# Seeding a PSUM bank from ScalarE instead of TensorE, and moving softplus's last sum from VectorE to TensorE in more tiles, in a selective-scan and mixture-of-experts layer

## What is computed

```
dt = softplus(ts @ W_dt.T + b_dt)
state = state * exp(dt * A) + (dt * u) * B        # u is x after convolution and silu
y = einsum(state, C)                              # over the 16 states
y = y + x * D                                     # the skip term
y = y * silu(gate)
s = y @ W_out.T
```

## Time and profile before

| | |
|---|---|
| three runs, median | 1090.31 us (1086.61 to 1090.49) |
| span of the profiled execution | 1086.8 us |
| time of the profiled execution outside the span | not in the profile; its span is 0.2 us above the fastest of the runs and 3.5 us below the median |
| mean granted clock of PE over the span | 0.911 of 2.4 GHz |
| chain that ended last, by engine | DVE 36%; PE 22%; POOL 15%; issue 12%; DMA 9%; ACT 4% |

### The profile page before, as it was taken

The page is one execution under the profiler, slowest core; times in us unless marked ns, Lnnn a source line. Parts: engine busy times, 40 slices in busy tenths (PEclk is TensorE's granted clock), DMA queues, the critical chain, the costliest instruction groups (busy, mean ns, idle before and its releaser), DMA issues.

```text
span 1086.8 us, 10255 instructions
## 1 busy us (share of the span) xinstructions
PE 872.1 (80%) x2774; PEld 323.8 (30%) x2774; DVE 1022.8 (94%) x1044; ACT 733.8 (68%) x1285; POOL 926.3 (85%) x365
## 2 busy tenths in 40 slices
PE   9944569798889998988656778989788997778576
PEld 5321123233223433333112223333223342223122
DVE  6779999999999999999999999899999999999998
ACT  3655567787787667766775667778767566676574
POOL 0629899999989889989889989798998978998995
PEclk9976788999989999999967879999999999799789
DMA  9355586556476665666743554766548566565714
GB/s 331 120 161 199 107 268 232 212 198 232 167 274 240 232 238 207 170 182 210 204 164 122 185 181 152 274 242 227 190 165 287 188 224 232 184 225 182 280 33 151
DMA packets 78089, 219.26 MB, mean 202 GB/s; under 512 B 15824, under 2 KB 17232, under 8 KB 71376
## 3 DMA queue, kind: packets, MB, share of 16 engines
q1 hardware_dynamic: 58096, 166.67, 44.7%
q10 hardware_dynamic: 12672, 31.46, 7.8%
q0 software_dynamic: 7264, 20.47, 6.9%
HBM read 176.85 MB, written 41.72 MB: 201 GB/s over the span
## 4 chain that ended last, share of the span: by engine, by line
DVE 36%; PE 22%; POOL 15%; issue 12%; DMA 9%; ACT 4%; SPq 2%; DVEq 0%; ACTq 0%; POOLq 0%
DVE sc_ps L1174 16%; POOL drive L567 10%; DVE drive L1174 6%; PE x_ps L1466 6%; DMA rep<-rep_rows 5%; DVE drive L1184 3%; PE f_ps L1419 3%; POOL drive L580 3%; PE y_ps L1434 3%; DMA x_slot<-xn_rows,slot_tok 2%; PE dt_ps L1394 2%; DVE x_ps L1113 2%; PE x_ps L1329 1%; PE x_ps L1351 1%; SPq L382 1%
## 5 line engine op out<-in xcount | busy, mean ns | idle before, releaser
L567 POOL TENSOR_TENSOR drive<-rep,b_all 128x2048 f32<-128x2048 f32 x127 | 575.8, 4538 | 44.1 <-DMA rep<-rep_rows 40.7
L799 ACT ACTIVATE sc_ps<-rep,a_neg 128x512 f32<-128x512 f32 x512 | 332.0, 681 | 86.2 <-DVE drive L1184 57.3
L1434 PE MATMUL y_ps<-drive,stack 128*32 128x512 f32 x1024 | 156.1, 687 | 89.7 <-DVE drive L1184 62.8
L1184 DVE TENSOR_TENSOR drive<-sc_ps,c_all 128x1024 f32<-128x1024 f32 x177 | 216.8, 1225 | 5.9
L1174 DVE TENSOR_TENSOR_SCAN sc_ps<-sc_ps,state,drive 128x512 f32<-128x512 f32 x178 | 218.4, 1273 | 3.8 <-ACT sc_ps L799 3.2
L1174 DVE TENSOR_TENSOR_SCAN sc_ps<-sc_ps,drive 128x512 f32<-128x512 f32 x176 | 205.3, 1212 | 5.5 <-ACT sc_ps L799 4.4
L580 POOL TENSOR_TENSOR drive<-drive,c_all 128x1024 f32<-128x1024 f32 x79 | 186.4, 2360 | 6.1 <-ACT state L778 6.1
L1419 PE MATMUL f_ps<-w_ring,xT_slot 128*128 128x512 f32 x368 | 176.5, 624 | 12.1 <-ACT xT_slot L811 12.1
L1394 PE MATMUL dt_ps<-xnT,w_g 128*128 128x512 f32 x232 | 117.8, 655 | 20.5 <-ACT dtu L766 20.4
L1419 PEld LDWEIGHTS f_ps<-w_ring,xT_slot 128*128 128x128 f32 x368 | 71.5, 201 | 118.3 <-issue 118.0
L1174 DVE TENSOR_TENSOR_SCAN drive<-sc_ps,state,drive 128x512 f32<-128x512 f32 x78 | 95.5, 1266 | 2.8 <-ACT sc_ps L799 2.8
(11 more groups left out here) (200 smaller groups left out, 1093.8 us busy)
## 6 DMA issues: line engine op xcount, KB each, us to landing
rep<-rep_rows SPq DMA_DIRECT2D x128, 512.0 KB, 6.7
w_ring<-wring SPq DMA_DIRECT2D x46, 1024.0 KB, 5.6
rep_rows<-dtu ACTq DMA_DIRECT2D x32, 512.0 KB, 3.3
slot_rows<-y_slot ACTq DMA_DIRECT2D x46, 256.0 KB
w_g<-wg_in SPq DMA_DIRECT2D x32, 256.0 KB, 2.7
w_x<-wx_in SPq DMA_DIRECT2D x24, 256.0 KB
xn_rows<-rep SPq DMA_DIRECT2D x16, 256.0 KB, 2.2
b_all<-bc_rows SPq DMA_DIRECT2D x16, 256.0 KB, 4.3
```

The costliest lines, as they stand in the source:

```text
L567: pool.tensor_tensor(drive[:, m % RING, :, :], rep[:, n % 2, :, 1, :], b_all[:, q:q + 1, :].broadcast_to([P, NR, TC]), ALU.mult).then_inc( ...
L799: act.activation(sc[:, r, :], rep[:, n % 2, r, 0, :], ACT.Exp, scale=a_neg[:, lo:lo + 1]).then_inc(decay_ok, 1)
L1184: dve.tensor_tensor(drive[:, m % RING, 2 * h:2 * h + 2, :], sc[:, 2 * h:2 * h + 2, :], c_all[:, q:q + 1, :].broadcast_to([P, 2, TC]), ALU. ...
L1434: last = pe.matmul(y_ps[CH * r:CH * (r + 1), :], stack[:, :], drive[:, m % RING, r, :], start=False, stop=(m % NQ == NQ - 1))
```

## The change

Three edits. The skip term is put into `y_ps` by one ACT instruction per tile (Copy with the scale D, 128x512), which waits for `gated`; PE waits for it (`skip_ok`) and then adds its sums onto it. Only tile 0 keeps the diagonal product. The Relu of a sum on PE is made in place in `dt_ps`, and PE adds three products onto it, not four onto a cleared bank. And `VECTOR_LOG` loses the tiles 2, 3, 16, 17, 19, 28, 29 and 31, so that 17 tiles, not 9, have their sum on PE.

```diff
-VECTOR_LOG = (0, 1, 2, 3, 4, 5, 7, 8, 10, 11, 12, 16, 17, 18, 19, 21, 23, 24, 26, 27, 28, 29, 31)
+VECTOR_LOG = (0, 1, 4, 5, 7, 8, 10, 11, 12, 18, 21, 23, 24, 26, 27)
...
                 if pe_log(k):
-                    act.activation(t_r[:, :], dt_ps[:, :], ACT.Relu).then_inc(relu_ok, 1)
+                    act.activation(dt_ps[:, :], dt_ps[:, :], ACT.Relu).then_inc(relu_ok, 1)
...
-            def diagonal(n):
-                if n:
-                    act.wait_ge(skip_mm, n)
-                act.activation(diag[:, :], ident[:, :], ACT.Copy, scale=dsk[:, n % NT:n % NT + 1]).then_inc(diag_ok, 1)
+            def diagonal():
+                act.activation(diag[:, :], ident[:, :], ACT.Copy, scale=dsk[:, 0:1]).then_inc(diag_ok, 1)
+
+            def skip(n):
+                if n == 0:
+                    return
+                c, t = divmod(n, NT)
+                act.wait_ge(gated, n)
+                act.activation(y_ps[:, :], xy[:, c % 2, t, :], ACT.Copy, scale=dsk[:, t:t + 1]).then_inc(skip_ok, 1)
...
-                diagonal(n)
+                if n == 0:
+                    diagonal()
                 if t < NT - 1:
                     keep_rows(n + 1)
...
                 decays(m + 1, 1)
+                skip(n)
                 copy_slot_T(b, first_slot)
...
-                pe.matmul(dt_ps[:, :], ident[:, :], t_e[:, :], start=True, stop=False)
-                pe.matmul(dt_ps[:, :], ident[:, :], t_w[:, :], start=False, stop=False)
-                pe.matmul(dt_ps[:, :], ident[:, :], t_l[:, :], start=False, stop=False)
-                pe.matmul(dt_ps[:, :], ident[:, :], t_r[:, :], start=False, stop=True).then_inc(log_mm, 1)
+                pe.matmul(dt_ps[:, :], ident[:, :], t_e[:, :], start=False, stop=False, skip_group_check=True)
+                pe.matmul(dt_ps[:, :], ident[:, :], t_w[:, :], start=False, stop=False, skip_group_check=True)
+                pe.matmul(dt_ps[:, :], ident[:, :], t_l[:, :], start=False, stop=True, skip_group_check=True).then_inc(log_mm, 1)
...
             def skip(n):
-                c, t = divmod(n, NT)
-                pe.wait_ge(diag_ok, n + 1)
                 if n:
-                    pe.wait_ge(gated, n)
-                pe.matmul(y_ps[:, :], diag[:, :], xy[:, c % 2, t, :], start=True, stop=False).then_inc(skip_mm, 1)
+                    pe.wait_ge(skip_ok, n)
+                    return
+                pe.wait_ge(diag_ok, 1)
+                pe.matmul(y_ps[:, :], diag[:, :], xy[:, 0, 0, :], start=True, stop=False)
```

More of the change, by code:

```diff
@@ L271, in scan_moe @@
         scaled, comb_ok, comb_last = sem("scaled"), sem("comb_ok"), sem("comb_last")
-        diag_ok, skip_mm = sem("diag_ok"), sem("skip_mm")
+        diag_ok, skip_ok = sem("diag_ok"), sem("skip_ok")
         x_mm, x_ev = sem("x_mm"), sem("x_ev")
@@ L1434, in sums @@
                     last = pe.matmul(y_ps[CH * r:CH * (r + 1), :], stack[:, :], drive[:, m % RING, r, :],
-                                     start=False, stop=(m % NQ == NQ - 1))
+                                     start=False, stop=(m % NQ == NQ - 1), skip_group_check=m >= NQ)
                 last.then_inc(sum_ok, 1)
```

## The result

The changed kernel took 1104.09 us, the median of 4 runs (1099.47 to 1104.93), against 1089.35 for the kernel before (1086.61 to 1090.49): a ratio of 1.0125, 95% interval 1.0098 to 1.0151. It is slower: the ratio, estimated from all the runs, gives 13.6 us, the medians 14.7. The forecast was 1100, slower, with 1082 to 1107 as its range. The profiled execution has a span of 1102.1 us, against 1086.8.

A forecast was written before the change was run, and what follows sets the result against it. DVE led at 94% busy, but the chain passed to POOL, `rep` and PE in places. Terms 0.7 + 3.4 + 3.3 + 4.0 = 11.4 us on 1086.8 gave 1098.2, put at 1100 us as the median; range 1082 to 1107.

The forecast's parts named there:

- DVE's 16.7 us: Three DVE instructions of 0.69 to 0.70 us leave each of eight tiles, 2.1 us a tile, 16.7 us in all.
- The rule of the most occupied engine: Trace-analysis advice to optimise the engine with highest occupancy first; by it the change is worth its DVE time.
- Tile 16, forecast +3.4: Sum made in tile 15 stands behind the gate's projection; DVE stands 8.6 us; +3.4 us (2 to 6).
- Tile 19, forecast +3.3: Sum made in tile 17 stands behind twelve out_tile products, moving the gate's projection, `rep` and POOL by +3.3 us.
- Tiles 2 and 3, +0.7: Sums made in tiles 0 and 1 at PE clock 0.50; dt of tile 2 later; +0.7 us (-2 to +2).
- tiles 28, 29, 31, +4.0: Sums in tiles 26 and 29 stand behind PE's sums waiting for POOL; +4.0 us (3 to 5.8).
- The skip term, forecast 0, from -3 to +4: ACT's seed fits its idle 0.71 us before the copy; expert products gain 0.1 us; counted 0, from -3 to +4.
- My fourth rival: Slower by more: seed keeps `y_ps` closed longer, 0.7 us a tile in half of 31, 11 us, 1111; chance 0.07.
- The faster one: DVE is the bound and its 16.7 us come off: 1073.6, or 1083 with half the stalls; chance 0.21 together.
- No change: Stalls as forecast but larger slack behind them, tiles 2, 3, 17 and 29 pay the rest: 1086 to 1095; chance 0.22.

The follow-up runs named there:

- e7: The kernel before with the changed kernel's 17 sums on PE and the in-place maximum, but the skip term still by diagonal product: 1094.48 us, ratio 1.0045.
- e11: The kernel before with 15 sums on PE (tiles 16 and 19 left on DVE), the in-place maximum and the diagonal product: 1088.45 us, ratio 0.9988.

## Why the prediction was right, and where it wasn't

The sign, the size (1104.1 against 1100) and, for tiles 16 and 19, the mechanism held: DVE came to wait at the places named, and these two stalls are most of the loss. The skip term and the price of the other six tiles did not hold. Step by step:

**DVE's 16.7 us.** 17.9 went, and its share fell to 91%. The waits for the last product rose by 18.3. The rule of the most occupied engine would have made the kernel faster; it is slower.

**Tile 16, forecast +3.4.** Right. The stall was 9.06 us against 8.6; gate 14 comes 7.1 us later than gate 13 did, and 3.7 of that are given back by gate 16: 3.4. Over the eight traces with this sum on PE it is 2.9 on average; the five without it gained 1.5, so the tile is worth 4.3 against the version without it, and 6.5 by putting it back, with an uncertainty of 4. The changed kernel's further 3.6 us at gate 13 are tile 12's, shown above; whether the seed or scatter brought them stays open.

**Tile 19, forecast +3.3.** Right by the traces: 2.9 us from gate 16 to gate 18 in the seven with it in its place, 0.2 in the five without. Putting it back gave 5.7, with the same uncertainty. Both tiles together are 10.0 us with the seed and 6.2 with the diagonal product (1.0045 less 0.9988), on the two sides of the 6.7 that I had summed; each is uncertain by 4, so that the seed makes these stalls dearer is possible and not shown.

**Tiles 2 and 3, +0.7, and tiles 28, 29, 31, +4.0.** The waits of 3.47 and 3.62 us at tiles 26 and 29 are where I said. But the six tiles other than 16 and 19 together cost 0.9 us with the seed, with an uncertainty of 4, and I had 4.7. The part on tiles 28, 29 and 31 is uncertain in itself: the traces with them on PE lost 3.4 us after gate 18 on average, from -4.0 to +10.2, those without 0.5, while the timed runs give 1.6 with an uncertainty of 5. Tile 17, whose sum had room, is in these six too.

**The skip term, forecast 0, from -3 to +4.** This is the step that failed. The runs put it at 2.7 to 8.7 us. I wrote that the seed fits into ACT's idle 0.71 us, from a tile whose transposes came late. There it does, but the products gain nothing: they begin 0.77 us after the transposes in both kernels, not 0.1 earlier. Where the transposes come early, ACT has no such idle time, the seed pushes the copy back, and the products begin 2.2 us after the gate instead of 1.6. And I asked what the diagonal product costs the path, not what PE does in its place. In the kernel before PE stands 20.7 us for the gate ahead of the diagonal products and 12.1 for the copy behind them, 32.8 in all; in the changed kernel it stands 52.9 in one piece each time, and behind the longest pieces the products run partly at 1.2 GHz. My fourth rival had the seed as the cause of a further loss, by 11 us through the sums that wait for `y_ps`. Those waits exist, 22.2 us of PE's weight loads in 7 places. No run separates them from the clock, so how the seed's cost divides between the two stays open.

So the total was near the mark partly because errors met: along one path from the kernel before to the changed one the runs give +2.7 for the seed, +0.9 for six tiles and +10.0 for two, 13.6 in all, where I had 0, 4.7 and 6.7. That the sum came out within 5 us of the measured time is in part luck.

**Rivals.** The faster one asked for stalls of tiles 15 and 17 under 4 us together; they are 9.06 and 5.34. "No change" asked for more slack behind them; there was less.

No version beat the kernel before. The nearest is e11, the diagonal product kept and tiles 16 and 19 left on DVE, at 0.9988 (0.9962 to 1.0013): the work it takes from DVE in six tiles is worth nothing that can be measured.

## What to carry to other kernels

Before work is moved off the fullest engine, look at each place for what stands ahead of it in the other engine's list, and for what the waiting engine wants first: here two places of eight made nearly the whole loss of the sums, and moving them ahead shortened one wait by 1.6 us and passed the other on to another consumer. A TensorE instruction that is off the path may still be worth its place when it splits an idle stretch between two bursts; before it is removed, read the idle time it would leave and the clock behind gaps of that size elsewhere in the same trace. One profiled execution shows mechanisms, but prices a place only if several traces of the same code agree.

## What was not expected of the hardware

With 31 products of about 1 us taken away from TensorE, others were slower: the expert products' mean is 652 ns in the changed kernel, 609 in e7 with the same sums, 14.7 us of busy time, and 624 in the kernel before. Behind idle stretches of 3.0 to 5.0 us the granted clock was low in 61 of 74 cases. And the first 213 us differ by up to 8.7 us at gate 3 between executions whose code up to there is alike.
